# A graph layer on one core: chunk sums taken a group further ahead with six sets of group buffers, and spread between the tiles' products

## The reference

```
h = x @ W_self.T + b_self + segment_sum(x[src] @ W_neigh.T + b_neigh, dst)
y = x + relu(h)
out = (y - mean(y)) / sqrt(var(y) + 1e-5)      # per node, over its 128 features
```

## Time and profile before

| | us |
|---|---|
| three runs | 694.75, 700.36, 702.02 |
| median | 700.36 |
| the profiled execution's own time | 693.77 |
| its span in the profile | 692.0 |

### The profile page before, as it was taken

How to read it: one execution, slowest core, us unless ns; L and a number is a source line. 1 busy time by engine, 2 the same in 40 slices (tenths; PEclk the granted TensorE clock), 3 DMA queues, 4 the chain that set the end, 5 groups by cost and what they waited for, 6 DMA issues and landing times.

```text
span 692.0 us, 12704 instructions
## 1 busy us (share of the span) xinstructions
PE 531.8 (77%) x3281; PEld 468.0 (68%) x3281; DVE 423.4 (61%) x1919; ACT 352.0 (51%) x1049; POOL 405.3 (59%) x424
## 2 busy tenths in 40 slices
PE   2046187878899769778877988888987897789895
PEld 0035076767778758667766867777877787678794
DVE  7883267688867657867747664644554535555564
ACT  1010055456555454655654655565655556456686
POOL 4777566666666645766557656656556656565400
PEclk9999589899798878988989989997789799888998
DMA  2422134444444454454443544444444434444443
GB/s 78 123 59 56 53 89 134 113 122 136 126 121 133 132 151 118 123 135 128 128 121 103 162 126 125 129 129 123 120 121 131 128 110 133 134 134 128 126 127 85
DMA packets 122942, 82.20 MB, mean 119 GB/s; under 512 B 15374, under 2 KB 115894, under 8 KB 122840
## 3 DMA queue, kind: packets, MB, share of 16 engines
q1 hardware_dynamic: 109208, 53.63, 27.5%
q0 software_dynamic: 13664, 27.77, 15.4%
HBM read 55.44 MB, written 26.71 MB: 119 GB/s over the span
## 4 chain that ended last, share of the span: by engine, by line
PE 61%; issue 15%; DVE 9%; another core or an unknown queue 6%; ACT 5%; DMA 2%; ACTq 1%; SPq 1%; POOL 0%; DVEq 0%
PE bank L889 17%; PE bank L912 16%; PE bank L913 13%; PE bank L877 6%; PE bank L908 5%; PE bank L894 3%; ACT result L1023 2%; DVE pick L730 2%; DVE y L740 2%; ACT sums_t L996 2%; DMA x_in<-in_x 1%; DVE below L530 1%; DMA end_dst<-in_dst 1%; ACT std L1013 1%
## 5 line engine op out<-in xcount | busy, mean ns | idle before, releaser
L482 POOL DMA_INDIRECT ring<-in_x,chunk_src x391 | 380.9, 974 | 236.3 <-issue 87.6
L996 ACT COPY sums_t<-bank 128x192 f32 x391 | 124.6, 319 | 290.5 <-remote 109.4
L889 PE MATMUL bank<-pick,ring 128*128 128x193 f32 (+1 forms) x782 | 188.8, 367 | 42.2 <-DVE pick L730 17.4
L912 PE MATMUL bank<-wsum_t,x_t 128*128 128x128 f32 (+1 forms) x782 | 188.3, 328 | 0.0
L913 PE MATMUL bank<-wn_t,sums_t 128*128 128x128 f32 (+1 forms) x782 | 174.5, 310 | 1.0 <-issue 0.9
L889 PEld LDWEIGHTS bank<-pick,ring 128*128 128x128 f32 x782 | 141.3, 215 | 49.5 <-issue 29.0
L1023 ACT ACTIVATE result<-y,minus_mean,rstd 128x128 f32<-128x128 f32 x391 | 163.5, 486 | 0.0
L912 PEld LDWEIGHTS bank<-wsum_t,x_t 128*128 128x128 f32 (+1 forms) x782 | 138.1, 221 | 26.8 <-issue 26.7
L740 DVE SCALAR_TENSOR_TENSOR y<-bank,x_in 128x384 f32<-128x384 f32 x131 | 72.6, 554 | 134.2 <-PE bank L913 65.2
L913 PEld LDWEIGHTS bank<-wn_t,sums_t 128*128 128x128 f32 (+1 forms) x782 | 141.1, 225 | 0.3 <-issue 0.2
L730 DVE TENSOR_SCALAR pick<-columns,local 128x194 f32<-128x194 f32 x391 | 106.3, 328 | 0.2
(11 more groups left out here) (118 smaller groups left out, 195.8 us busy)
## 6 DMA issues: line engine op xcount, KB each, us to landing
x_in<-in_x SPq DMA_DIRECT2D x130, 192.0 KB
out<-result SPq DMA_DIRECT2D x130, 192.0 KB
ring<-in_x,chunk_src POOLq DMA_INDIRECT x391
degrees_t<-degrees_dram SPq DMA_DIRECT2D x130, 2.2 KB
dst_padded<-in_dst SPq DMA_DIRECT2D x1, 390.6 KB
src_padded<-in_src SPq DMA_DIRECT2D x1, 390.6 KB
edge_src<-in_src SPq DMA_DIRECT2D x1, 390.6 KB
edge_dst<-in_dst SPq DMA_DIRECT2D x1, 390.6 KB
```

Source lines behind the costliest of these rows:

```text
L482: nc.gpsimd.indirect_dma_start(ring[:, c % RING, :], None, x, bass.IndirectOffsetOnAxis(ap=chunk_src[:, c:c + 1], axis=0)).then_inc(gather ...
L889: ins = mm(into[:, frame:frame + SPAN + carried], ring[:, c % RING, :], pick[tau % DEEP][:, c % TRIO, 0:SPAN + carried], start=(c == 0), s ...
L912: mm(h, x_t[b][:, q, 0:rows], k.wsum_t[:], start=False, stop=False)
L996: nc.scalar.copy(sums_t[:, bass.ds(at, SPAN)], sum_bank[c // PAIR % SUM_BANKS][:, frame:frame + SPAN]).then_inc(sums_placed, 1)
```

## The change

`DEEP` is 6 instead of 4: six buffers of all that it counts, SP's loads up to six groups ahead instead of four, and its stores eight groups behind its loads instead of six. From group 3 on (`RAMP`) `sums_ahead(t)` is what group t + 1 needs, and two more: 3t + 13 chunks, three per step, no longer rounded. ACT places whole pairs of these only.

PE's step t is now: transposes of group t + 1; bias product of group t; any sum that is still missing for it; and then for each of the three tiles one chunk's sum and the tile's two products. The wait for placed sums stands in front of the first tile's products, behind the first of these sums. ACT copies x_t of group t + 1 first and then places sums, and writes the result of group t - 4 instead of t - 3. DVE takes the reciprocal and the scaled mean of group t - 3 instead of t - 2. No arithmetic is added or left out.

```diff
-DEEP = 4
+DEEP = 6
+RAMP = 3
 def whole_pairs(chunks):
-    return min(CHUNKS, -(-chunks // PAIR) * PAIR)
+    return chunks if chunks == CHUNKS else chunks // PAIR * PAIR
 def sums_ahead(trio):
-    return whole_pairs(sums_needed(min(trio, TRIOS - 1)) + PAIR)
+    return min(CHUNKS, sums_needed(min(trio + (trio >= RAMP), TRIOS - 1)) + PAIR)
...
-            for t in range(TRIOS + 2):
+            for t in range(TRIOS + 3):
...
-                if 2 <= t < TRIOS + 2:
-                    invert(t - 2)
+                if t >= 3:
+                    invert(t - 3)
                 if 1 <= t <= TRIOS:
                     aggregate(t - 1)
-                if 2 <= t < TRIOS + 2:
-                    scale_mean(t - 2)
+                if t >= 3:
+                    scale_mean(t - 3)
...
-            def products(tau):
+            def first_product(tau):
                 b = tau % 2
                 tiles, rows = tiles_of(tau)
                 pe.wait_ge(degrees_landed[tau % DEEP], 16 * (tau // DEEP + 1))
                 pe.wait_ge(xt_copied, tau + 1)
                 if tau >= 2:
                     pe.wait_ge(y_done, tau - 1)
-                pe.wait_ge(sums_placed, sums_needed(tau))
-                if tau in joined_at:
-                    pe.wait_ge(laps_joined, joined_at[tau])
                 mm(h_bank[b][0:rows, 0:tiles * DIM], degrees_t[tau % DEEP][:, 0:rows], k.bias[:, 0:tiles, :], start=True, stop=False)
-                for q in range(tiles):
-                    h = h_bank[b][0:rows, q * DIM:q * DIM + DIM]
-                    at = (tau * TRIO + q) * P % LAP
-                    mm(h, x_t[b][:, q, 0:rows], k.wsum_t[:], start=False, stop=False)
-                    ins = mm(h, sums_t[:, at:at + rows], k.wn_t[:], start=False, stop=(q == tiles - 1))
-                ins.then_inc(h_done, 1)
+
+            def tile_products(tau, q):
+                b = tau % 2
+                tiles, rows = tiles_of(tau)
+                h = h_bank[b][0:rows, q * DIM:q * DIM + DIM]
+                at = (tau * TRIO + q) * P % LAP
+                if q == 0:
+                    pe.wait_ge(sums_placed, sums_needed(tau))
+                    if tau in joined_at:
+                        pe.wait_ge(laps_joined, joined_at[tau])
+                mm(h, x_t[b][:, q, 0:rows], k.wsum_t[:], start=False, stop=False)
+                ins = mm(h, sums_t[:, at:at + rows], k.wn_t[:], start=False, stop=(q == tiles - 1))
+                if q == tiles - 1:
+                    ins.then_inc(h_done, 1)
...
             for t in range(TRIOS):
                 later_lists(t)
-                while summed < sums_ahead(t):
+                if t + 1 < TRIOS:
+                    turn_x(t + 1)
+                first_product(t)
+                tiles = tiles_of(t)[0]
+                while whole_pairs(summed) < sums_needed(t):
                     sum_chunk(summed)
                     summed += 1
-                if t + 1 < TRIOS:
-                    turn_x(t + 1)
-                products(t)
+                ahead = sums_ahead(t) - summed
+                for q in range(tiles):
+                    for _ in range(ahead * (q + 1) // tiles - ahead * q // tiles):
+                        sum_chunk(summed)
+                        summed += 1
+                    tile_products(t, q)
...
-            for t in range(TRIOS + 3):
-                while placed < sums_ahead(t):
+            for t in range(TRIOS + 4):
+                if t + 1 < TRIOS:
+                    copy_x_t(t + 1)
+                while placed < whole_pairs(sums_ahead(t)):
                     place_sums(placed)
                     placed += 1
-                if t + 1 < TRIOS:
-                    copy_x_t(t + 1)
                 if 2 <= t < TRIOS + 2:
                     deviation(t - 2)
-                if t >= 3:
-                    normalise(t - 3)
+                if t >= 4:
+                    normalise(t - 4)
```

## The result

The changed kernel took 690.04 us (median of 4 runs, 687.41 to 695.95), the kernel before 700.94 beside it: ratio 0.9892, 95% interval [0.9848, 0.9936]. (The ratio is estimated over the runs; it isn't the quotient of the two medians, which is 0.984.) The 690.04 us are inside the forecast's range (638 to 706), but the gain is a third of the one forecast. Measured again in the course of the experiments it was 0.9924 [0.9879, 0.9970] on a chip where the kernel before takes 688.78 us, and **1.0119 [1.0088, 1.0150]** on one where it takes 560.48. Two of the nine runs behind the 688.78 us were slow ones, which the ratios leave out; the median of the other seven is 685.60. The lower level, about 561 us, is what four of the five chips of the experiments gave.

What follows compares the result with a forecast made beforehand. POOL's gathers and its pauses on a full ring were taken to bound the kernel. 692.0 - 23 - 5.5 + 2 + 3 = 668.5 us of span, 670.3 of execution, 677 on the median's scale; range 638 to 706.

Steps and rivals of the forecast that it cites:

- What bounds the kernel: The loop is POOL's gathers (498 us) and its pauses on a full ring (113 us), plus 5 us of odd waits.
- four chunks per pause: In POOL's pauses for PE: sums ahead let PE do four chunks per pause, so 92 pauses instead of 116, -23 us.
- rival B: No change, 700 us: PE's stops are its own time, or each pause only grows with gathers before it; chance 0.18.
- the single bank of transposes: At PE's transposes of the next group: waiting for ACT's copy to empty the bank limits PE to four chunks per pause.
- lose most of their cause: At PE's bias product: the 31 + 9 stops on placed sums, 51.0 us, mostly go because sums are made a group ahead.
- Start +2: At the loop's start: the first sums now wait behind the bias product for the degrees; +2 us, between 0 and +10.
- End +3: Behind the last gather: one more group's products and one further ACT result remain; +3 us.
- One sum between products, 0: In PE's step: the same matmuls in another order, none added; 0 us.
- Six buffers' x_in, -5.5: Near 250 us: loading x two groups earlier removes PE's 5.5 us wait for x_in; -5.5 us.
- A: Rival: signals stop mattering, PE gets two steps per pause, -54 us instead of -23, 646 us; chance 0.22.
- C: Rival: ACT's three results delay its x_t copy, each pause grows by 1.25 us; slower, +50 us, 727 us; chance 0.18.

Runs made afterwards that it cites:

- plain loads: The changed kernel with ordinary loads of 128 consecutive rows from SP's queue in place of each gather: 544.29, 546.63, 544.98 and 545.86 us.
- bursts of six: The kernel before, with POOL asking for free slots only at every sixth gather, then for six: 561.73 us (1.0016) on one chip, 729.25 (1.0598) on another.
- breather: The kernel before with a memset of one column on POOL behind each gather: 562.15 us against 560.90, 1.0026.

## Why the prediction was wrong

**What bounds the kernel: right at 700 us.** Gathers, POOL's pauses, start and end add up in both profiles, above. Where signals are prompt, the same sum without pauses, 391 x 1.28 = 500 us from 38.3 on, gives the end of the last gather at 539, where 540.3 was measured.

**The reading of the bound had a flaw that fed the failed step.** I took 2.96 us for PE's step, from 671.72 to 674.68. But PE takes four sums in one step and two in the next, and this was a step of two. The y's ahead of these in the same trace of the kernel before:

```profile
661.11 0.56 DVE L740 SCALAR_TENSOR_TENSOR y<-bank,x_in 128x384 f32<-128x384 f32 x1 [0.33 <-PE bank L913]
665.22 0.55 DVE L740 SCALAR_TENSOR_TENSOR y<-bank,x_in 128x384 f32<-128x384 f32 x1
667.89 0.56 DVE L740 SCALAR_TENSOR_TENSOR y<-bank,x_in 128x384 f32<-128x384 f32 x1 [0.24 <-PE bank L913]
```

4.11, 2.67, 3.83, 2.96: two steps take 6.79 us, one **3.39**. In the changed kernel the y's behind the last gather stand at 652.31 and 662.51, three steps of three sums each, 3.40. The kernel with plain loads, in which PE is busy for 97% of the time at full clock, gives no less: 402.28 us of busy time over its 2900 matmuls are 3.4 us for the 24.8 of a group (3252 in 131 groups). So PE has 3.82 - 3.39 = 0.43 us to spare in a group, not 0.86. A stop of 2 us takes it some five groups to make up at full clock, and it spends part of them at half (6.72 us after the stop above).

**The failed step: "four chunks per pause. So 367 / 4 = 92 pauses instead of 116, -24 x 0.98 = -23 us".** It forecast a fall of 23 us and 4.6 came, because neither the count nor the price went as it says. The 116 pauses include the one stop of 5.9 us at the x_in loads, which I counted again as -5.5; without it the ordinary pauses cost 115 x 0.94 = 107.7 us before and 100 x 1.03 = 103.1 after. The missing 18.4 us are, by size:

- **The price per pause, about 9.4 us** (100 x 0.094). I kept it at 0.98. On the like count it rose from 0.94 at 115 pauses to 1.03 at 100; it was 0.96 at 106 on the other chip, and 2.48 at 60 in the bursts of six. That is the second half of rival B, "each pause only grows with the number of gathers before it". A reason that fits, and that no run isolates: PE has half the spare time that I gave it, so work left undone in a burst stays undone until POOL stops.
- **The number, about 7.5 us** (8 x 0.94). It fell to 100, and to 106 on the other chip, not to 92. What I named as next, the single bank of transposes, is it: PE's stops there, 65.6 us over 58, stand in the place of most of the 68.4 us that PE waited at the bias product and for picks. Nor did the stops on placed sums "lose most of their cause": 50.8 us in 39 stops became 20.4 in 26 between 100 us and the last gather. Which instruction PE stops at hardly mattered.
- **The stop counted twice, about 1.5 us**: it raised the mean price from 0.94 to 0.98 and the count by one.

**The other terms held.** Start +2: the first sums are placed at 62.17 and the pauses come at 76.5 and 80.1 us, 4.9 us above the gap for both, in place of the 5.04 at 86.52; the kernel with the missing sums in front of the bias product bounds the rest at 4 us, for 561 us only. End +3: 4.8 in the profiles at 700 us, 3.4 at 561. One sum between products, 0: 3.40 against 3.39 us a step. Six buffers' x_in, -5.5: -5.6 in this pair of profiles; the second profile at that level shows that PE can still wait 3.3 us for x_in.

**The rivals.** A is out: one transposed bank was enough to hold the signals' effect, and POOL's waits stayed at 133. C named the wait that came and its cause (in the stop shown, ACT's results stand in front of the copy), but not its price: the stops at the transposes took the place of others and were not added to them, 87.3 us of waits in all before and 83.8 after. B, "nothing is there to win", was the nearest in size at 700 us: the pauses gave 4.6 us of 113. Its first half, that the stops are PE's own time, has against it that the same matmuls on another chip are followed by DVE and ACT after 0.04 and 0.11 us, not about 2, and the record of PE's signals above. The Trainium skill, "Perfetto Trace Analysis", section "Tensor Engine Instruction (MATMUL, LD_WEIGHTS)", says that a matmul's end in the records is an estimate; by that rule alone the 2 us would be there on every chip, and the traces speak against it.

**What no step held at all** is that signals can be prompt. There the change has nothing to remove and still pays its end, 3.4 us of the 3.7 by which the spans differ: 1.2% slower over the runs. No rival was that. Why the signals are late on some occasions isn't settled: the gathers take as long there (0.974 to 0.979 us) as elsewhere (0.978 in the breather), they were never taken away on such a chip, and neither part of the change was run alone on one. The profiles put more of the gain on the stop at the x_in loads (-5.6 us) than on all ordinary pauses (-4.6). Which part of the change brings either is not shown.

## What to carry to other kernels

A count of waits times their mean price is a forecast only if the price doesn't depend on the count; where an engine pays at a stop for what it left undone, look at the total, and at how much spare time per step it has to catch up. Take that spare time from as many steps as the schedule's pattern has, here two, and look for a stop that stands in two terms. Time such a change on more than one chip: here it gave -1.1%, -0.8% and +1.2%.

## What the runs showed of the hardware

One program has two levels. The kernel before took 700 us at first, 689 on one chip of the experiments, and 560.5 to 561.6 on the four others. What the traces show to differ is how soon TensorE's signals come: 324 of 557 more than 0.5 us late while POOL gathers, against none of 632 over 0.02 us. Other engines act on them after about 2 us or after 0.04 and 0.11. At the higher level too they are prompt behind the last gather (0.30 and 0.33 us of idle on DVE, and 0.01 us at the median of the recorded signals), so there the lateness goes with the time of the gathers; on the four chips the same gathers do no such harm.

Half clock followed an idle PE in both places looked at: 0.50 for 6.72 us after 2.26 us of idle, 0.5 for 3.41 us after 2.39. With the gathers gone PE ran 413 us at 1.00. The Trainium skill, "TensorE: Matmul & The Clock Gate", Part 1, calls half clock the default that activity lifts; these three stretches agree.

POOL's 0.30 us between two indirect DMAs hides a memset of 0.12 us entirely.
